# Taking DRAIN instructions out of the PSUM evacuation of a feed-forward stage, and one buffer for its bias broadcast

## The chip, the cores and the metric

The kernel runs on all 8 cores of one Trainium2 chip. Each core handles its own 2048 tokens (half a sequence of one of 4 batch entries), and nothing is exchanged between cores. The metric is the device time in microseconds of the slowest core; lower is better.

## What is computed

A pre-norm transformer layer on x of shape 4 x 4096 x 1024:

```python
x = x + attn(layernorm(x), Wq, Wk, Wv, Wo)        # 16 heads, rotary, full softmax
x = x + ffn(layernorm(x), w1, b1, w2, b2)
# ffn: two "bitlinear" layers, 1024 -> 4096 -> 1024, exact gelu between them
def bitlinear(x, w, b):
    xq = act_quant(rmsnorm(x))      # rounded to -128..127 by the row's max
    wq = weight_quant(w)            # rounded to -1, 0, 1
    return einsum('bsd,fd->bsf', xq, wq) + b
```

## The kernel before, in words

The program is written by hand, with one instruction stream per engine and named semaphores. It has five stages with a barrier of all engines between them (`barrier_all`, line 116): row statistics, the projections to K, Q and V, attention (the exponential at L686), the output projection with the quantization of w2, and the feed-forward stage. Only this last stage is touched. Its code begins at line 1016.

**Where it starts.** b1 (4096 numbers) and b2 (1024) have to stand in all 128 partitions (`b1_bc`, `b2_bc`). This is done in five pieces of 1024 numbers: GpSimd loads a piece of 4 KB to row 0 of `outb` (L1082), TensorE multiplies it by a column of ones (two fp32 matmuls, L1115 and L1118 for even pieces, L1123 and L1126 for odd ones), and VectorE copies the two halves from PSUM (L1138, L1139 or L1142, L1143). Two rows (`outb[0]`, `outb[1]`) and two PSUM places (`ps4_b1`, `ps4_b2`) take turns. GpSimd's stream goes on with the loads of the first tiles of its tokens, `y1t` (512 KB each, L1086 and L1092).

**The loop over 16 token tiles of 128.** For tile t TensorE runs, in this order: 8 transposes of the quantized input of tile t+1 (L1303, "A transposes"), 32 transposes of the quantized hidden row of tile t (L1323, "B transposes"), 64 matmuls of the first layer of tile t+1 (L1290: 8 blocks of 512 columns, 8 matmuls each), 64 matmuls of the second layer of tile t (L1338). All transposes share three PSUM slots, `ps4_tr`: transpose g waits in `wait_slot` until transpose g-3 has been copied out. VectorE copies the A transposes (`ev1_copies`, L1173) and the odd B transposes (`ev2_odd`, L1246), ScalarE the even B transposes (L1385).

VectorE's stream for tile t is: two quantizing passes over a quarter of the hidden row (L1251, L1260), two more, the 8 A copies, 4 odd B copies, a quarter's passes, 4 copies, a quarter's passes, 8 copies; then the output of tile t-1 (`do_out`, L1202); then for each of the 8 blocks of the first layer the scale and bias out of PSUM (`hstt_range`, L1183) and, two blocks behind, the maximum over the block after gelu (`mx8_one`, L1209); then the quantized input of tile t+2 (`q1_round`, L1153 to L1166) and a chain of six small operations. ScalarE runs gelu (L1376) and the sum of squares (L1379) for each block.

**How an instruction tells that it is done.** Nearly everywhere on VectorE and ScalarE the instruction is followed by a separate `e.drain()`, and the semaphore's increment hangs on that drain. A helper such as `ev1_copies` reads

```python
e.wait_ge(SM["pTE"], gq1(t, i) + 1)
e.tensor_copy(q1fm[:, i * 128:(i + 1) * 128], ps4_tr[gq1(t, i) % 3][:])
e.drain().then_inc(SM["vTE"], 1)
```

The exception is the exponential of the attention stage (L686), which carries its increment itself.

Of the kernel before, what the change touches and what calls it, by code (L numbers as in the profile page):

```python
# [11 lines left out]
AF = mybir.ActivationFunctionType  # L12
ALU = mybir.AluOpType
# [16 lines left out]
def build_nc():  # L30
# [14 lines left out]
    b1r = din("b1r", [1, FF])  # L45
    b2r = din("b2r", [1, D])
# [10 lines left out]
    with st_all:  # L57
# [4 lines left out]
        def mkp(stack, name, shape, dtype=F32):  # L62
# [15 lines left out]
            "vQ2", "vQ2c", "pL2", "dBb", "vOU", "dOUa", "dOUb",  # L78
        ]
        SM = {n: st_all.enter_context(nc.semaphore(n)) for n in SEMS}  # L80

# [3 lines left out]
        ones_f1 = mk(st_all, "ones_f1", [1, 128])  # L85
# [941 lines left out]
        ps4_b2 = mkp(st4, "ps4_b2", [128, 1024])  # L1027
# [46 lines left out]

        @block.gpsimd
        def _(e):
            for cc in range(5):
                if cc >= 2:
                    e.wait_ge(SM["pIC"], cc - 1)
                src = (b1r[0:1, cc * 1024:(cc + 1) * 1024] if cc < 4  # L1080
                       else b2r[0:1, :])
                e.dma_start(out=outb[cc % 2][0:1, 0:1024],  # L1082
                            in_=src).then_inc(SM["dB" if cc % 2 == 0
                                                 else "dBb"], 16)
            for t in range(2):
# [20 lines left out]
        @block.tensor  # L1106
        def _(e):
            for cc in range(5):
                e.wait_ge(SM["dB" if cc % 2 == 0 else "dBb"],
                          16 * (cc // 2 + 1))  # L1110
                bdst = b1_bc if cc < 4 else b2_bc
                if cc >= 2:
                    e.wait_ge(SM["vC2"], cc - 1)
                if cc % 2 == 0:
                    e.matmul(ps4_b1[0][:], ones_f1[:],  # L1115
                             outb[0][0:1, 0:512],
                             start=True, stop=True, skip_group_check=True)
                    e.matmul(ps4_b1[1][:], ones_f1[:],  # L1118
                             outb[0][0:1, 512:1024],
                             start=True, stop=True,  # L1120
                             skip_group_check=True).then_inc(SM["pIC"], 1)
                else:
                    e.matmul(ps4_b2[:, 0:512], ones_f1[:],  # L1123
                             outb[1][0:1, 0:512],
                             start=True, stop=True, skip_group_check=True)
                    e.matmul(ps4_b2[:, 512:1024], ones_f1[:],  # L1126
                             outb[1][0:1, 512:1024],
                             start=True, stop=True,
                             skip_group_check=True).then_inc(SM["pIC"], 1)

        @block.vector
        def _(e):
            for cc in range(5):
                e.wait_ge(SM["pIC"], cc + 1)
                bdst = b1_bc if cc < 4 else b2_bc
                off = cc * 1024 if cc < 4 else 0
                if cc % 2 == 0:
                    e.tensor_copy(bdst[:, off:off + 512], ps4_b1[0][:])  # L1138
                    e.tensor_copy(bdst[:, off + 512:off + 1024],  # L1139
                                  ps4_b1[1][:])  # L1140
                else:
                    e.tensor_copy(bdst[:, off:off + 512], ps4_b2[:, 0:512])  # L1142
                    e.tensor_copy(bdst[:, off + 512:off + 1024],  # L1143
                                  ps4_b2[:, 512:1024])
                e.drain().then_inc(SM["vC2"], 1)

        @block.vector
        def _(e):
# [21 lines left out]
            def ev1_copies(t):  # L1170
                for i in range(NDC):
                    e.wait_ge(SM["pTE"], gq1(t, i) + 1)
                    e.tensor_copy(q1fm[:, i * 128:(i + 1) * 128],  # L1173
                                  ps4_tr[gq1(t, i) % 3][:])
                    e.drain().then_inc(SM["vTE"], 1)

            def hstt_range(t, fcs):
                for fc in fcs:
                    g = 8 * t + fc
                    e.wait_ge(SM["pL1"], g + 1)  # L1180
                    if g >= 2:
                        e.wait_ge(SM["aGE"], g - 1)
                    e.scalar_tensor_tensor(hb[g % 2][:], ps4_b1[fc % 2][:],  # L1183
                                           c1o_t[:, t:t + 1],
                                           b1_bc[:, fc * 512:(fc + 1) * 512],
                                           ALU.mult, ALU.add)
                    e.drain().then_inc(SM["vIC"], 1)

            RRS = ["rr", "ssq"]

# [30 lines left out]
            for t in range(NTTQ):  # L1221
# [138 lines left out]
        def _(e):  # L1360
# [9 lines left out]
            for t in range(NTTQ):  # L1370
# [101 lines left out]
```

## Time and profile before

| what | us |
|---|---|
| two runs, lowest and highest | 2822.35 and 2880.93 |
| their median | 2851.64 |
| the profiled execution | 2826.34 |
| its span, slowest core (core 0) | 2824.7 |
| spans of the eight cores | 2804.1 to 2824.7 |
| feed-forward stage of core 0 | about 2070 to 2824.7 |

A row of the timeline gives the start, the duration, the engine, the line, the operation, the output and inputs, how many instructions are merged in the row and, in brackets, how long the engine had been idle and what ended that. PE is TensorE's matmul, PEld its weight load, DVE VectorE, ACT ScalarE, POOL GpSimd. A releaser with a q, such as DVEq, is an instruction of the engine's sequencer, here mostly a drain. "issue" is time in which the engine waited for nothing that the profile shows.

### The profile page before, as it was taken

The page shows a single profiled execution, that of the slowest core. Times are in us where ns is not written, and L with a number is a line of the kernel's source. Part 1 is how long each engine was busy: PE and PEld are TensorE (multiplying, and loading weights), DVE is VectorE, ACT ScalarE, POOL GpSimd, SP SyncE. Part 2 cuts the span into 40 slices and gives each one's busy share as a digit, 9 for nine tenths or more (in the row PEclk, how much of TensorE's full clock was granted, in tenths as well). Part 3 has the DMA queues.
Part 4 walks back from the last instruction along what each step waited for, and adds up shares of the span by engine and source line. Part 5 has one row for each costly group of instructions (what it writes and reads, how often), then busy time and mean ns, then how long its engine had stood idle before and what let it go on. Part 6 is the DMA issues. An engine that isn't in the chain of part 4 may idle for free.

```text
span 2824.7 us, 33066 instructions; the slowest of 8 cores (2804.1 to 2824.7 us)
## 1 busy us (share of the span) xinstructions
PE 2212.6 (78%) x8854; PEld 759.8 (27%) x8940; DVE 1067.9 (38%) x1941; ACT 1600.0 (57%) x2139; POOL 181.1 (6%) x345
## 2 busy tenths in 40 slices
PE   4679999788888888888888888554047888888887
PEld 1223333222222222222222222121013333334333
DVE  2424445401111111101122220188555666666664
ACT  3301111399888999889998889411433443434432
POOL 4211111000000000000000000011110000000000
PEclk8799999898898998888988889777567988889888
DMA  9632323301101010101111110366520000000000
GB/s 159 96 60 60 60 58 72 103 16 30 53 30 45 23 53 31 53 1 45 45 45 62 39 36 6 80 220 207 189 71 16 16 31 16 31 23 23 31 16 23
DMA packets 72194, 160.57 MB, mean 57 GB/s; under 512 B 8144, under 2 KB 41040, under 8 KB 70736
## 3 DMA queue, kind: packets, MB, share of 16 engines
q0 software_dynamic: 48544, 104.90, 16.0%
q1 hardware_dynamic: 23472, 53.55, 5.3%
q8 instruction: 80, 1.31, 0.2%
q14 instruction: 98, 0.80, 0.1%
HBM read 158.42 MB, written 29.36 MB: 66 GB/s over the span
## 4 chain that ended last, share of the span: by engine, by line
PE 40%; ACT 28%; DVE 11%; issue 11%; DMA 6%; DVEq 1%; ACTq 1%; POOL 0%; POOLq 0%; SPq 0%
ACT Et L686 25%; PE ps_b L1290 8%; PE ps_b L1338 8%; PE ps_k L405 5%; PE ps_v L380 4%; PE ps_tr L1323 3%; DMA xb<-x_fm 3%; PE ps_cA L621 2%; PE ps_S L656 2%; PE ps_cB L627 2%; DMA w2st<-w2T 2%; DVE wtmp L878 1%; DVE q1fm L1173 1%; PE ps_k L412 1%; PE ps_n L421 1%
## 5 line engine op out<-in xcount | busy, mean ns | idle before, releaser
L686 ACT ACTIVATE Et<-ps_S,negG 128x1024 bf16<-128x1024 f32 x1024 | 1046.8, 1172 | 85.0 <-PE ps_S L661 77.7
L656 PE MATMUL ps_S<-Qp,Kp 64*128 64x512 bf16 x1024 | 411.7, 407 | 122.9 <-ACT Et L686 72.5
L621 PE MATMUL ps_cA<-Et,V_sb 128*65 128x512 bf16 x1024 | 436.6, 426 | 43.1 <-DVEq L768 36.6
L661 PE MATMUL ps_S<-Qp,Kp 64*128 64x512 bf16 x1024 | 423.3, 418 | 0.0
L627 PE MATMUL ps_cB<-Et,V_sb 128*65 128x512 bf16 x1024 | 413.9, 404 | 0.0
L756 DVE COPY rlbc<-ps_rl 64x512 f32<-64x512 f32 x32 | 21.8, 682 | 768.3 <-PE ps_rl L638 768.3
L1290 PE MATMUL ps_b<-w1q,q1fm 128*128 128x512 bf16 x992 | 251.1, 417 | 7.3 <-issue 5.2
L656 PEld LDWEIGHTS ps_S<-Qp,Kp 64*128 64x128 bf16 x1024 | 93.5, 94 | 597.3 <-issue 597.2
L493 ACT ACTIVATE ksq<-krot 128x512 bf16<-128x512 bf16 x96 | 60.4, 629 | 298.0 <-DVEq L461 298.0
L1338 PE MATMUL ps_b<-w2q,q2fm 128*128 128x512 bf16 x1007 | 225.0, 382 | 3.3 <-DVEq L1205 2.4
L621 PEld LDWEIGHTS ps_cA<-Et,V_sb 128*65 128x65 bf16 x1024 | 113.5, 111 | 301.2 <-issue 294.6
L1385 ACT ACTIVATE q2fm<-ps_tr 128x128 bf16<-128x128 bf16 x256 | 70.9, 277 | 194.3 <-PE ps_tr L1323 193.8
L1323 PE MATMUL ps_tr<-eye_b,h_scb 128*128 128x128 bf16 x512 | 114.9, 252 | 77.3 <-DVEq L1248 51.6
L1290 PEld LDWEIGHTS ps_b<-w1q,q1fm 128*128 128x128 bf16 x1024 | 106.9, 106 | 146.6 <-issue 50.7
L979 PE MATMUL ps_y<-wo_b,ctx_fm 128*128 128x512 bf16 x250 | 80.4, 490 | 74.1 <-DVEq L863 50.3
L1338 PEld LDWEIGHTS ps_b<-w2q,q2fm 128*128 128x128 bf16 x1024 | 100.6, 98 | 124.9 <-issue 5.7
L380 PE MATMUL ps_v<-wv_b,xr 128*128 128x512 bf16 x496 | 115.0, 383 | 18.1 <-DMA xr<-x_fm 16.6
L1183 DVE SCALAR_TENSOR_TENSOR hb<-ps_b,c1o_t,b_bc 128x512 f32<-128x512 f32 x128 | 96.1, 751 | 85.1 <-PE ps_b L1290 66.8
L627 PEld LDWEIGHTS ps_cB<-Et,V_sb 128*65 128x65 bf16 x1024 | 119.3, 117 | 6.6
L405 PE MATMUL ps_k<-xr,wk_b 128*128 128x512 bf16 x504 | 119.8, 381 | 1.3 <-issue 1.3
L596 POOL DMA_DIRECT2D w1st_<-w1T x64 | 33.8, 528 | 1157.2 <-DVEq L716 630.7
L1209 DVE TENSOR_REDUCE mx<-h_sc 128x1 f32<-128x512 f32 x128 | 87.8, 686 | 23.4 <-issue 18.0
(199 smaller groups left out, 2152.5 us busy)
## 6 DMA issues: line engine op xcount, KB each, us to landing
w1st_<-w1T POOLq DMA_DIRECT2D x64, 512.0 KB, 4.2
w2st<-w2T POOLq DMA_DIRECT2D x64, 512.0 KB, 4.6
xb<-x_fm POOLq DMA_DIRECT2D x64, 128.0 KB, 9.6
xr<-x_fm POOLq DMA_DIRECT2D x64, 128.0 KB, 6.0
kscr<-krot SPq DMA_DIRECT2D x64, 128.0 KB, 1.9
Kp<-kscr SPq DMA_DIRECT2D x8, 1024.0 KB, 4.8
xq<-x_tmq SPq DMA_DIRECT2D x16, 512.0 KB, 5.9
y1scr<-y1r SPq DMA_DIRECT2D x16, 512.0 KB, 5.1
```

Source lines behind the costliest of these rows:

```text
L380: e.matmul(ps1_v[j % 2][:, h * 512:(h + 1) * 512], xr[bi % 2][:, c * 512 + t4 * 128: c * 512 + t4 * 128 + 128], wv_b[:, c * 1024 + h * 512 ...
L405: mm = e.matmul(ps1_k[idx % 2][:], wb[:, c * 1024 + mdo * 128:c * 1024 + mdo * 128 + 128], xr[bi % 2][:, c * 512:(c + 1) * 512], start=(c ...
L621: e.matmul(ps2_cA[:], V_sb[:, jj * VBLK + (2 * m) * VW: jj * VBLK + (2 * m) * VW + VW], Et[itp % 4][:, 0:512], start=(jj == 0), stop=(jj = ...
L627: e.matmul(ps2_cB[:], V_sb[:, jj * VBLK + (2 * m + 1) * VW: jj * VBLK + (2 * m + 1) * VW + VW], Et[itp % 4][:, 512:1024], start=(jj == 0), ...
L656: e.matmul(ps2_S[it % 2][:, 0:512], Kp[m % 2][0:64, j * 128:(j + 1) * 128], Qp[m % 2][0:64, qh * 512:(qh + 1) * 512], start=True, stop=Tru ...
L661: e.matmul(ps2_S[it % 2][:, 512:1024], Kp[m % 2][64:128, j * 128:(j + 1) * 128], Qp[m % 2][64:128, qh * 512:(qh + 1) * 512], start=True, s ...
L686: e.activation(Et[it % 4][:], ps2_S[it % 2][:], AF.Exp, bias=negG[:, m:m + 1], scale=1.0).then_inc(SM["aEX"], 1)
L1183: e.scalar_tensor_tensor(hb[g % 2][:], ps4_b1[fc % 2][:], c1o_t[:, t:t + 1], b1_bc[:, fc * 512:(fc + 1) * 512], ALU.mult, ALU.add)
L1209: e.reduce_max(mx8[:, fc:fc + 1], h_sc[:, fc * 512:(fc + 1) * 512], axis=AX, apply_absolute_value=True)
L1290: last = e.matmul(ps4_b1[fc % 2][:], q1fm[:, c * 128:(c + 1) * 128], w1q[:, c * FF + fc * 512:c * FF + (fc + 1) * 512], start=(c == 0), st ...
L1323: e.transpose(ps4_tr[g % 3][:], h_scb2[k % 2][:, (i % 8) * 128: (i % 8 + 1) * 128], eye_b[:]).then_inc(SM["pTE"], 1)
L1338: last = e.matmul(ps4_b2[:, h2 * 512:(h2 + 1) * 512], q2fm[:, fc * 128:(fc + 1) * 128], w2q[:, fc * 1024 + h2 * 512: fc * 1024 + (h2 + 1) ...
```

## The change

Three things, all in the feed-forward stage.

1. The drain is removed after the A copies, the odd and the even B copies and the `hstt_range` operation, and the increment is put on the operation itself; behind `mx8_one`'s reduction, which carries none, the drain goes without replacement. Over 16 tiles that is 128 drains after A copies, 256 after odd B copies, 128 after L1183 and 128 after L1209 on VectorE, and 256 after even B copies on ScalarE.
2. The bias pieces use `outb[0]` and `ps4_b1` alone. The load of piece cc waits until VectorE has copied piece cc-1 out of PSUM (`vC2`).
3. The first two loads of `y1t` stand ahead of the bias loads in GpSimd's stream.

```diff
@@ gpsimd
-            for cc in range(5):
-                if cc >= 2:
-                    e.wait_ge(SM["pIC"], cc - 1)
...
-                e.dma_start(out=outb[cc % 2][0:1, 0:1024],
-                            in_=src).then_inc(SM["dB" if cc % 2 == 0
-                                                 else "dBb"], 16)
             for t in range(2):
                 e.dma_start(out=y1t[t % 3][:],
...
+            for cc in range(5):
+                if cc >= 1:
+                    e.wait_ge(SM["vC2"], cc)
...
+                e.dma_start(out=outb[0][0:1, 0:1024],
+                            in_=src).then_inc(SM["dB"], 16)
@@ tensor
-                e.wait_ge(SM["dB" if cc % 2 == 0 else "dBb"],
-                          16 * (cc // 2 + 1))
+                e.wait_ge(SM["dB"], 16 * (cc + 1))
-                if cc >= 2:
-                    e.wait_ge(SM["vC2"], cc - 1)
...
@@ ev1_copies (the same in ev2_odd, in hstt_range and in ScalarE's copy)
                     e.tensor_copy(q1fm[:, i * 128:(i + 1) * 128],
-                                  ps4_tr[gq1(t, i) % 3][:])
-                    e.drain().then_inc(SM["vTE"], 1)
+                                  ps4_tr[gq1(t, i) % 3][:]
+                                  ).then_inc(SM["vTE"], 1)
@@ mx8_one
                 e.reduce_max(mx8[:, fc:fc + 1],
                              h_sc[:, fc * 512:(fc + 1) * 512], axis=AX,
                              apply_absolute_value=True)
-                e.drain()
```

On GpSimd, at the start of the stage, the loads stand in this order before; `outb0` and `outb1` are the two bias rows, `pIC` counts pieces that TensorE has multiplied.

```order
L1075 UNCONDITIONAL_BRANCH [waits sBAR]
L1082 DMA outb0<-b1r 1x16x64
L1082 DMA outb1<-b1r 1x16x64
L1082 DMA outb0<-b1r 1x16x64 [waits pIC]
L1082 DMA outb1<-b1r 1x16x64 [waits pIC]
L1082 DMA outb0<-b2r 1x16x64 [waits pIC]
L1086 DMA y1t0<-y1scr 128x1024
L1086 DMA y1t1<-y1scr 128x1024
L1092 DMA y1t2<-y1scr 128x1024
```

The same place of the changed kernel; `vC2` counts pieces that VectorE has copied out.

```order
L1075 UNCONDITIONAL_BRANCH [waits sBAR]
L1078 DMA y1t0<-y1scr 128x1024
L1078 DMA y1t1<-y1scr 128x1024
L1086 DMA outb0<-b1r 1x16x64
L1086 DMA outb0<-b1r 1x16x64 [waits vC2] x3
L1086 DMA outb0<-b2r 1x16x64 [waits vC2]
L1091 DMA y1t2<-y1scr 128x1024
```

Two large loads have moved ahead of the bias, and four of the five bias loads now wait for VectorE instead of three for TensorE.

On TensorE, at the same place, the broadcasts before alternate between two PSUM places:

```order
L1106 UNCONDITIONAL_BRANCH [waits sBAR]
L1115 MATMUL ps4_b10<-outb0,ones_f1 128x512 [waits dB]
L1118 MATMUL ps4_b11<-outb0,ones_f1 128x512
L1123 MATMUL ps4_b2<-outb1,ones_f1 128x512 [waits dBb]
L1126 MATMUL ps4_b2<-outb1,ones_f1 128x512
L1115 MATMUL ps4_b10<-outb0,ones_f1 128x512 [waits dB,vC2]
L1118 MATMUL ps4_b11<-outb0,ones_f1 128x512
```

and in the changed kernel every piece goes through the same one:

```order
L1110 MATMUL ps4_b10<-outb0,ones_f1 128x512 [waits dB]
L1112 MATMUL ps4_b11<-outb0,ones_f1 128x512
L1110 MATMUL ps4_b10<-outb0,ones_f1 128x512 [waits dB]
L1112 MATMUL ps4_b11<-outb0,ones_f1 128x512
L1110 MATMUL ps4_b10<-outb0,ones_f1 128x512 [waits dB]
```

The number of matmuls is the same; each pair waits for a load that is itself behind the copies of the pair before. In the loop over tiles no instruction other than the drains changes its place on any engine.

## Rows read from the trace of the kernel before

**Rows 1.** TensorE's timeline through one tile; start, duration, instruction, idle before.

```profile
2493.90 15.79 PE L1290 MATMUL ps_b<-w1q,q1fm 128*128 128x512 bf16 x62 [0.36 <-issue]
...
2523.34 0.33 PE L1303 MATMUL ps_tr<-eye_b,uscr_b 128*128 128x128 bf16 x3
...
2524.48 0.22 PE L1303 MATMUL ps_tr<-eye_b,uscr_b 128*128 128x128 bf16 x1 [0.19 <-DVEq L1175]
...
2530.99 2.12 PE L1323 MATMUL ps_tr<-eye_b,h_scb 128*128 128x128 bf16 x8 [1.54 <-DVEq L1248]
...
2538.19 2.34 PE L1290 MATMUL ps_b<-w1q,q1fm 128*128 128x512 bf16 x5 [0.34 <-issue]
```

**Rows 2.** Windows: stretch, its length, busy time by engine, TensorE's granted clock, DMA.

```profile
2070.00:2092.00 22.00, 17.40 (x20) 6.33 (x20) 6.73 (x11) 0.00 (x0) 4.03 (x8) 0.50 0.21 72
...
2523.30:2538.20 14.90, 8.71 (x42) 4.02 (x42) 8.29 (x28) 4.43 (x16) 0.00 (x0) 0.68 0.00 1
```

**Rows 3.** VectorE's timeline between the matmuls of that tile.

```profile
2523.66 0.23 DVE L1173 COPY q1fm<-ps_tr 128x128 bf16<-128x128 bf16 x1 [0.45 <-PE ps_tr L1303]
...
2524.08 0.22 DVE L1173 COPY q1fm<-ps_tr 128x128 bf16<-128x128 bf16 x1 [0.19 <-issue]
...
2524.49 0.22 DVE L1173 COPY q1fm<-ps_tr 128x128 bf16<-128x128 bf16 x1 [0.19 <-PE ps_tr L1303]
...
2528.45 0.23 DVE L1246 COPY q2fm<-ps_tr 128x128 bf16<-128x128 bf16 x1 [0.21 <-PE ps_tr L1323]
...
2528.80 0.75 DVE L1251 TENSOR_SCALAR h_sc<-h_sc,scr 128x1024 f32<-128x1024 f32 x1
```

**Rows 4.** Timeline of the w2 quantization: two operations with a drain between, GpSimd behind them.

```profile
2057.77 0.69 DVE L932 TENSOR_SCALAR w2st<-w2st 128x1024 f32<-128x1024 f32 x1 [1.18 <-ACTq L967]
2058.55 0.70 DVE L935 TENSOR_SCALAR w2q<-w2st 128x1024 bf16<-128x1024 f32 x1
...
2059.82 0.53 POOL L829 DMA_DIRECT2D w2st<-w2T  x1 [2.12 <-DVEq L937]
```

**Rows 5.** Timeline of the bias broadcast: GpSimd, TensorE, VectorE.

```profile
2070.68 0.98 POOL L1082 DMA_DIRECT2D outb<-b1r  x2 [7.65 <-DVEq L119]
...
2072.72 2.04 PE L1115 MATMUL ps_b<-outb,ones_f 1*128 1x512 f32 x2 [88.16 <-DMA outb<-b1r]
...
2076.58 0.69 DVE L1138 COPY b_bc<-ps_b 128x512 f32<-128x512 f32 x1 [6.59 <-PE ps_b L1118]
...
2077.19 0.68 DVE L1139 COPY b_bc<-ps_b 128x512 f32<-128x512 f32 x1
...
2091.71 0.55 DVE L1153 TENSOR_SCALAR uscr<-y1t,c1q_t,kmag_t 128x512 f32<-128x512 f32 x1 [0.19 <-issue]
```

**Rows 6.** Costliest groups: the exponential, whose increment is on the instruction itself.

```profile
L686 ACT ACTIVATE Et<-ps_S,negG 128x1024 bf16<-128x1024 f32 x1024 | 1046.8, 1172 | 85.0 <-PE ps_S L661 77.7
```

**Rows 7.** Attention stage's timeline: two exponentials and the matmul that waits for the second.

```profile
999.06 2.15 ACT L686 ACTIVATE Et<-ps_S,negG 128x1024 bf16<-128x1024 f32 x2
...
1001.36 0.37 PE L656 MATMUL ps_S<-Qp,Kp 64*128 64x512 bf16 x1
```

**Rows 8.** The two loads of line 1086, from issue to landing.

```profile
DMA to landing us min/median/max: 3.6/4.3/5.0
```

**Rows 9.** Where weight loads become dense again after three starts of matmuls (with those starts).

```profile
2098.92 15.50 PE L1290 MATMUL ps_b<-w1q,q1fm 128*128 128x512 bf16 x62 [1.11 <-DVEq L1175]
...
2102.18 10.03 PEld L1290 LDWEIGHTS ps_b<-w1q,q1fm 128*128 128x128 bf16 x47 [0.16 <-issue]
...
2137.68 3.57 PE L1290 MATMUL ps_b<-w1q,q1fm 128*128 128x512 bf16 x8
...
2143.10 7.22 PEld L1290 LDWEIGHTS ps_b<-w1q,q1fm 128*128 128x128 bf16 x34 [0.20 <-issue]
...
2498.09 9.38 PEld L1290 LDWEIGHTS ps_b<-w1q,q1fm 128*128 128x128 bf16 x44 [0.20 <-issue]
```

**Rows 10.** TensorE's timeline: its wait for VectorE in the first tile.

```profile
2123.84 1.91 PE L1303 MATMUL ps_tr<-eye_b,uscr_b 128*128 128x128 bf16 x5 [9.24 <-DVEq L1175]
```

More of the change, by code:

```diff
@@ L77, in build_nc @@
             "vQ1", "pTE", "vTE", "vTEB", "vTEBD", "pL1", "aGE", "aSQ", "vSF", "aC2", "vC2",
-            "vQ2", "vQ2c", "pL2", "dBb", "vOU", "dOUa", "dOUb",
+            "vQ2", "vQ2c", "pL2", "vOU", "dOUa", "dOUb",
         ]
@@ L1076, in _ @@
         def _(e):
-            for cc in range(5):
-                if cc >= 2:
-                    e.wait_ge(SM["pIC"], cc - 1)
-                src = (b1r[0:1, cc * 1024:(cc + 1) * 1024] if cc < 4
-                       else b2r[0:1, :])
-                e.dma_start(out=outb[cc % 2][0:1, 0:1024],
-                            in_=src).then_inc(SM["dB" if cc % 2 == 0
-                                                 else "dBb"], 16)
             for t in range(2):
@@ L1088, in _ @@
                             ).then_inc(SM[["dYLa", "dYLb", "dYLc"][t % 3]], 16)
+            for cc in range(5):
+                if cc >= 1:
+                    e.wait_ge(SM["vC2"], cc)
+                src = (b1r[0:1, cc * 1024:(cc + 1) * 1024] if cc < 4
+                       else b2r[0:1, :])
+                e.dma_start(out=outb[0][0:1, 0:1024],
+                            in_=src).then_inc(SM["dB"], 16)
             for t in range(2, NTTQ):
@@ L1108, in _ @@
             for cc in range(5):
-                e.wait_ge(SM["dB" if cc % 2 == 0 else "dBb"],
-                          16 * (cc // 2 + 1))
+                e.wait_ge(SM["dB"], 16 * (cc + 1))
                 bdst = b1_bc if cc < 4 else b2_bc
-                if cc >= 2:
-                    e.wait_ge(SM["vC2"], cc - 1)
[L1114 to L1129, printed above, removed]
+                e.matmul(ps4_b1[0][:], ones_f1[:], outb[0][0:1, 0:512],
+                         start=True, stop=True, skip_group_check=True)
+                e.matmul(ps4_b1[1][:], ones_f1[:], outb[0][0:1, 512:1024],
+                         start=True, stop=True,
+                         skip_group_check=True).then_inc(SM["pIC"], 1)
         @block.vector
@@ L1136, in _ @@
                 off = cc * 1024 if cc < 4 else 0
[L1137 to L1144, printed above, removed]
+                e.tensor_copy(bdst[:, off:off + 512], ps4_b1[0][:])
+                e.tensor_copy(bdst[:, off + 512:off + 1024], ps4_b1[1][:])
                 e.drain().then_inc(SM["vC2"], 1)
@@ L1185, in hstt_range @@
                                            b1_bc[:, fc * 512:(fc + 1) * 512],
-                                           ALU.mult, ALU.add)
-                    e.drain().then_inc(SM["vIC"], 1)
+                                           ALU.mult,
+                                           ALU.add).then_inc(SM["vIC"], 1)
             RRS = ["rr", "ssq"]
@@ L1246, in ev2_odd @@
                         e.tensor_copy(q2fm[:, i * 128:(i + 1) * 128],
-                                      ps4_tr[gq2(t, i) % 3][:])
-                        e.drain().then_inc(SM["vTEBD"], 1)
+                                      ps4_tr[gq2(t, i) % 3][:]
+                                      ).then_inc(SM["vTEBD"], 1)
                 for k in range(4):
@@ L1385, in _ @@
                     e.activation(q2fm[:, i * 128:(i + 1) * 128],
-                                 ps4_tr[gq2(t, i) % 3][:], AF.Copy)
-                    e.drain().then_inc(SM["vTEB"], 1)
+                                 ps4_tr[gq2(t, i) % 3][:],
+                                 AF.Copy).then_inc(SM["vTEB"], 1)
         @block.sync
@@ L1393, in _ @@
             e.wait_ge(SM["dYLc"], 16 * 5)
-            e.wait_ge(SM["dB"], 16 * 3)
-            e.wait_ge(SM["dBb"], 16 * 2)
+            e.wait_ge(SM["dB"], 16 * 5)
         st4.close()
```

## The prediction

> **What bounds the kernel now.** I read the timeline of one late tile first, engine by engine, then the windows for TensorE's clock, then the start of the feed-forward stage. Everything before that stage is untouched, so only the last 750 us count.
>
> A tile takes 2538.19 - 2493.90 = 44.3 us from first matmul to first matmul [rows 1]. TensorE multiplies without a break from 2493.90 to 2523.34, 29.4 us, and then needs 14.85 us for 40 transposes. The reader should see that the second part is not TensorE's own work: single transposes stand 0.2 to 1.5 us apart and a DVE drain released them. The mechanism is the ring of three PSUM slots: a transpose may start only when the one three before it has been copied out. Behind the first three transposes the copies on VectorE follow each other every 0.41 us, 0.22 of copy and 0.19 in which the engine idles with "issue" as its reason, that is, for its own drain and the wait instruction behind it [rows 3]. TensorE then waits 1.54 us for the first odd B copy after two quantizing passes [rows 1, 3].
>
> TensorE's granted clock is part of this. In the transposes it is 0.68 on average [rows 2]: at 2.4 GHz for (0.68 - 0.5) / 0.5 = 36% of 14.9 us, so it falls to 1.2 GHz about 5.4 us after the matmuls end, and the next matmuls begin at 1.2 GHz and regain 2.4 GHz only 4.2 us later, where the weight loads become dense (2493.90 to 2498.09) [rows 1, 9].
>
> The start of the stage is a chain of its own: from the first bias load at 2070.68 to the end of the last bias copy, just before 2091.71, about 20.8 us [rows 5], at 1.2 GHz throughout [rows 2]. TensorE is busy for 17.4 of these 22 us: the two PSUM places keep it fed, and loads and copies lie beside it. No tile can start before it.
>
> **The change part by part.**
>
> *The bias in one buffer.* Now each piece runs load, multiply, copy, and only then the next load. From rows 5: GpSimd's issue to TensorE's start 2072.72 - 2070.68 = 2.04; TensorE's start to VectorE's first copy 2076.58 - 2072.72 = 3.86; the two copies start 0.61 apart and the second takes 0.68, 1.29 together. From VectorE's end to a load on GpSimd that waits for its drain: 2059.82 - (2058.55 + 0.70) = 0.57 [rows 4]. One round is 2.04 + 3.86 + 1.29 + 0.57 = 7.76; a later load may land a tenth or two sooner, so I take 7.7. Four rounds are 30.8, and the fifth piece ends with 3.86 + 1.29 = 5.15.
>
> *The y1t loads ahead of it.* They cost their issue on GpSimd, two of about 0.55 us, and perhaps their transfer. From the stage's start to the first bias matmul: at least 1.1 + 2.04 = 3.1 us if the small load passes them, and 0.55 + 5.0 + 0.1 = 5.7 if it lands behind the second large one [rows 8]. There the third large load was competing, so I take 5.0. The new start is then 5.0 + 30.8 + 5.15 = 41 us against 20.8: **+20 us**, with bounds +16 (first load early, rounds 7.2) and +23. Nothing hides it: VectorE's bias copies stand ahead of the first tile in its stream. The early y1t saves nothing, since tile 0 did not wait for it: its first operation followed the copies by 0.19 of issue [rows 5].
>
> The page DMA: Bandwidth & Descriptors of the Trainium skill (Queues, rings and completion order) says that a semaphore write of a DMA engine lands only behind that engine's earlier writes, across its queues. By that rule the small load is counted behind both large ones, which is the upper of my two ends; no row of this trace has a small load issued behind large ones on the same queue.
>
> *The A copies.* What does a copy without its drain cost? The same engine shows both forms on plain operations: with a drain between them L932 and L935 start 0.78 apart at a duration of 0.69 [rows 4]; the bias copies L1138 and L1139, with neither drain nor wait, start 0.61 apart at 0.69 [rows 5], so the second starts 0.08 before the first ends. A wait between two instructions need not break this: the exponentials on ScalarE carry their own increments, have two waits between them, and two of 1.17 us each take 2.15 together [rows 6, 7]. So the 0.19 gap should go. Then the slot ring sets the pace: copy 0.22, copy's end to the next transpose 0.15, transpose's start to its copy 2523.66 - 2523.34 = 0.32 [rows 1, 3], together 0.70 for three slots, 0.23 each. The 0.15 is from the exponential to the matmul it releases, 1001.36 - (999.06 + 2.15) [rows 7]; with a drain it is 2524.48 - 2524.30 = 0.18 [rows 1, 3]. Eight A copies save 8 x (0.41 - 0.23) = 1.4 us per tile. What is late next is the ring itself.
>
> *The odd and even B copies.* Here 8 transposes already take 2.12 us, 0.265 each [rows 1]: the ring binds, not the drains. The shorter handshake saves 0.03 / 3 = 0.01 on each, for some 20 of them 0.2. At two places per tile VectorE goes from an odd copy to the quantizing pass on which the next transposes depend; that gap, 2528.80 - 2528.68 = 0.12 [rows 3], turns into an overlap of 0.08: 2 x 0.2 = 0.4.
>
> Sum per tile: 1.4 + 0.2 + 0.4 = **2.0 us**. From both sides: 0 if wait and increment take as long as the drain did, and 8 x (0.41 - 0.14) + 0.4 + 0.5 = 3.0 if copies could run at 0.22 - 0.08 = 0.14 without regard to the ring. I take 2.0 because both terms are read at this very place.
>
> *L1183 and L1209.* Their drains stand while TensorE multiplies without a break, so that TensorE hides whatever they save in 15 tiles. If that cover were gone, it would be 0.2 x 16 = 3.2 us a tile, but it would need TensorE to wait in the matmuls, and it doesn't. Tile 0 is different: no second-layer matmuls cover VectorE there, and TensorE waits 9.24 us [rows 10]. I put the saving at 1.4 (0.9 because the last L1183 no longer trails, and three gaps of 0.15 to 0.2).
>
> *The clock.* The matmuls will start 2 us sooner, but whether 2.4 GHz returns sooner too is open: after three starts it came back after 3.3, 5.4 and 4.2 us [rows 1, 9]. A microsecond more at 1.2 GHz costs half of one. I subtract 0.3 per tile; the spread of the three, 3.3 to 5.4 against 4.2, allows -0.45 to +0.6.
>
> **Sum.** 15 tile intervals x (2.0 - 0.3) = 25.5; tile 0 another 1.4, its first A copies 1.4, the last tile (B transposes only) 0.6: 28.9 saved, 20 added, **-9 us**. The profiled execution took 2826.34, its span 2824.7. Forecast: 2826.3 - 9 = **2817 us**. That execution lies near the lower of the two runs shown (2822.35 and 2880.93) and 25 us below their median; the forecast is for an execution like it.
>
> **The rivals.**
>
> *The drains were free.* Wait and increment may take their 0.19 anyway, and the copies keep their pace. For it: no row shows VectorE with an increment on the operation and a wait behind it. Against it: rows 6 and 7 on ScalarE, and 0.61 against 0.78 in rows 5 and 4. Then only the bias chain is left, with handshakes saving some 2 us: 2826.3 + 20 - 2 = 2844, slower than before. It decides wherever the saving stays under 1.2 us per tile, which is the 20 us over 16.5 tiles. The Trainium skill's page VectorE: DVE Perf Modes (The DRAIN you can't avoid) states this very case: eight copies took the same time with a semaphore after each as with one after the last, since each operation drains anyway. The bias copies, 0.61 apart, don't show such a wait; by that rule the result would be this rival's.
>
> *The clock keeps half.* If 2.4 GHz returns at the moment it would have returned anyway, 2 us more at 1.2 GHz give back 1.0 a tile: 15 x 1.0 + 3.4 = 18.4 saved, 2826.3 + 20 - 18.4 = 2828. For it: the three returns do not follow the start by one fixed time. Against: nothing ties them to a place in the old schedule.
>
> *The clock stays up.* If the denser transposes kept 2.4 GHz, each start would save 4.2 / 2 = 2.1 more: 15 x (2.0 + 2.1) + 3.4 = 65, 2826.3 + 20 - 65 = 2781. Against it: in the last third of the gap 8 transposes still take about 2 us and VectorE's passes still leave TensorE idle for over a microsecond twice.
>
> **How the numbers follow.** Forecast 0.5, drains free 0.18, clock keeps half 0.2, clock stays up 0.05, and 0.07 for an execution like the higher of the two shown. The bounds of the terms give 2826 + 23 - 0 = 2849 as the slow end and 2826 + 16 - (15 x 3.0 + 5) = 2792 as the fast one; with part of the spread of the two runs above it the range is **2796 to 2860**. Within 2% (about what a measurement of this kernel can tell from no change) lie all cases but a part of the last two: 0.94. Faster 0.03, slower 0.03.
>
> **What would show it.** Right: five bias rounds of about 7.7 us with GpSimd's loads waiting for VectorE, the first tile starting 20 us later; A copies 0.23 apart with TensorE as their releaser; the B ring still near 0.26; tiles 42 to 43 us apart; a granted clock that still falls to 0.5 in every gap. Wrong: copies still 0.41 apart (drains free), tiles of 43.3 or more with the first matmuls at 0.5 for over 5.5 us (the clock's share), tiles near 40 with no 0.5 (the clock stays up), or a bias start under 36 us.

## The result and the profile after

| what | us |
|---|---|
| changed kernel, median of 24 runs (lowest, highest) | 2811.7 (2799.6, 2883.6) |
| kernel before, median of 23 runs beside them | 2826.4 |
| ratio of the two, with its 95% interval | 0.9938 (0.9913 to 0.9962) |
| that ratio in us | -17.5 (-24.6 to -10.7) |
| profiled execution of the changed kernel | 2808.8 |
| forecast | 2817, which is -9 |

It is a little faster and within 2%, as forecast, but by about twice as much. Medians and extremes are over all runs; some runs, of the kernel before too, are a few per cent longer at a lower granted clock on one die or both, and the ratios, and the times given for e4 and e7 below, leave those out. The profile says where the gain lies. The slowest core is now core 3:

```profile
span 2807.2 us, 32253 instructions; the slowest of 8 cores (2785.5 to 2807.2 us)
```

All rows below are of core 0 where nothing else is said, so that they can be laid beside the rows of before. Line numbers have moved: the bias loads are now L1086, the bias copies L1122 and L1123, the first operation of a tile L1132, the A copies L1152, the odd and even B copies L1224 and L1363, the transposes L1281 (A) and L1301 (B), the first-layer matmuls L1268.

**The start.** The timeline of GpSimd, TensorE and VectorE answers to [rows 5]:

```profile
2069.10 1.05 POOL L1078 DMA_DIRECT2D y1t<-y1scr  x2 [7.46 <-DVEq L119]
2070.14 0.50 POOL L1086 DMA_DIRECT2D outb<-b1r  x1
2074.35 2.04 PE L1110 MATMUL ps_b<-outb,ones_f 1*128 1x512 f32 x2 [90.36 <-DMA outb<-b1r]
...
2078.20 0.69 DVE L1122 COPY b_bc<-ps_b 128x512 f32<-128x512 f32 x1 [9.77 <-PE ps_b L1112]
...
2080.08 0.49 POOL L1086 DMA_DIRECT2D outb<-b1r  x1 [9.44 <-DVEq L1124]
2082.05 2.04 PE L1110 MATMUL ps_b<-outb,ones_f 1*128 1x512 f32 x2 [3.96 <-DMA outb<-b1r]
...
2110.08 0.55 DVE L1132 TENSOR_SCALAR uscr<-y1t,c1q_t,kmag_t 128x512 f32<-128x512 f32 x1 [0.19 <-issue]
```

GpSimd's second bias load is released by VectorE's drain (DVEq L1124), and TensorE, which was busy almost throughout before, waits 3.96 us for it. The first matmul comes 5.25 us after the first issue (forecast 5.0), the second round starts 7.70 later (7.7; the other three take 7.52, 7.57 and 7.60), and the first tile begins 2110.08 - 2069.10 = 41.0 us after the first issue (41). Against 21.0 before that is 20 us lost, on all eight cores (20.9 to 22.2 before, 40.8 to 41.7 now).

**Between the matmuls.** The timeline of one late tile, TensorE and VectorE together, answers to [rows 1] and [rows 3]:

```profile
2517.67 0.33 PE L1281 MATMUL ps_tr<-eye_b,uscr_b 128*128 128x128 bf16 x3
2517.99 0.49 DVE L1152 COPY q1fm<-ps_tr 128x128 bf16<-128x128 bf16 x3 [2.09 <-PE ps_tr L1281]
...
2518.36 0.48 PE L1281 MATMUL ps_tr<-eye_b,uscr_b 128*128 128x128 bf16 x3 [0.37 <-DVE q1fm L1152]
2518.68 0.49 DVE L1152 COPY q1fm<-ps_tr 128x128 bf16<-128x128 bf16 x3 [0.21 <-PE ps_tr L1281]
...
2519.06 0.35 PE L1281 MATMUL ps_tr<-eye_b,uscr_b 128*128 128x128 bf16 x2 [0.21 <-DVE q1fm L1152]
2519.38 0.36 DVE L1152 COPY q1fm<-ps_tr 128x128 bf16<-128x128 bf16 x2 [0.20 <-PE ps_tr L1281]
...
2521.50 0.23 DVE L1224 COPY q2fm<-ps_tr 128x128 bf16<-128x128 bf16 x1 [0.33 <-PE ps_tr L1301]
2521.64 0.74 DVE L1229 TENSOR_SCALAR h_sc<-h_sc,scr 128x1024 f32<-128x1024 f32 x1
...
2523.78 0.52 PE L1301 MATMUL ps_tr<-eye_b,h_scb 128*128 128x128 bf16 x3 [1.42 <-DVE q2fm L1224]
...
2530.61 14.78 PE L1268 MATMUL ps_b<-w1q,q1fm 128*128 128x512 bf16 x62 [0.34 <-issue]
```

Three copies of 0.22 now stand in one row of 0.49, so they start 0.13 apart, and then VectorE waits for TensorE, not for itself. The groups of three start at 2517.99, 2518.68 and 2519.38: the ring of three slots turns in 0.69 to 0.70 us, the 0.70 of the forecast. Behind an odd copy the quantizing pass starts 0.09 before the copy ends (forecast 0.08). The gap is 2530.61 - 2517.67 = 12.94. Its mean over tiles 2 to 14 is 12.85 against 14.82, on every core within 0.02: **1.97 us shorter, forecast 2.0**. The means here and below run from the first weight load of the A transposes to the first of the matmuls, because on two cores, core 0 among them, some matmul rows are missing (x62 of 64).

**The clock.** Windows of 100 us from the middle of the stage, after and then before (columns as in [rows 2]; the last but two is TensorE's granted clock):

```profile
2300.00:2400.00 100.00, 86.13 (x389) 39.38 (x393) 62.02 (x151) 41.13 (x101) 1.05 (x2) 0.86 0.06 22
2400.00:2500.00 100.00, 86.91 (x388) 39.91 (x396) 61.78 (x140) 44.24 (x106) 1.58 (x3) 0.85 0.09 32
2500.00:2600.00 100.00, 89.64 (x411) 41.24 (x418) 65.79 (x147) 44.31 (x105) 1.05 (x2) 0.90 0.06 22
```

```profile
2300.00:2400.00 100.00, 83.03 (x367) 37.24 (x371) 63.06 (x143) 39.18 (x98) 1.05 (x2) 0.84 0.06 22
2400.00:2500.00 100.00, 84.88 (x362) 37.60 (x369) 61.83 (x135) 40.33 (x97) 1.58 (x3) 0.82 0.09 32
2500.00:2600.00 100.00, 86.83 (x382) 38.73 (x388) 64.53 (x134) 45.58 (x109) 1.05 (x2) 0.86 0.06 22
```

The clock has become better, 0.87 against 0.84 in the mean, where I had counted a loss. Counted over whole tiles (2 to 14, all cores), TensorE is at 1.2 GHz for 11.3 us of a tile against 13.6. How much of it falls into the matmuls can be read, as in [rows 9], from a start of matmuls and the place where the weight loads become dense. After, three neighbouring tiles:

```profile
2404.52 14.68 PE L1268 MATMUL ps_b<-w1q,q1fm 128*128 128x512 bf16 x62 [0.34 <-issue]
2406.23 12.47 PEld L1268 LDWEIGHTS ps_b<-w1q,q1fm 128*128 128x128 bf16 x58 [0.28 <-issue]
...
2445.75 14.51 PE L1268 MATMUL ps_b<-w1q,q1fm 128*128 128x512 bf16 x54 [0.34 <-issue]
2450.81 9.16 PEld L1268 LDWEIGHTS ps_b<-w1q,q1fm 128*128 128x128 bf16 x43 [0.22 <-issue]
...
2488.84 15.18 PE L1268 MATMUL ps_b<-w1q,q1fm 128*128 128x512 bf16 x62 [0.34 <-issue]
2491.77 11.75 PEld L1268 LDWEIGHTS ps_b<-w1q,q1fm 128*128 128x128 bf16 x55 [0.22 <-issue]
```

1.7, 5.1 and 2.9 us. Counted instead from the first weight load, which lies 0.4 us ahead of these matmul rows, to the clock's own record, it is 2.3, 5.4 and 3.3 us. By this count the matmuls spend 2.0 to 5.6 us at 1.2 GHz over tiles 2 to 14 of all cores, 3.5 in the mean; before it was 2.8 to 4.6, 4.2 in the mean, and 4.1 to 4.6 from tile 6 on. A tile now takes 41.98 us (mean of tiles 2 to 14 over the cores) against 44.30: 1.97 from the gap and 0.35 from the matmuls (0.5 on core 0).

### The profile page after: what moved, and what is told of

Its sections match the earlier page's. It is cut to its first block, busy times and chain, and to the rows that moved or that the text cites. A ratio compares the mean times of both kernels' runs of the same rounds, so it can differ in the third digit from the quotient of the medians.

```text
span 2807.2 us, 32253 instructions; the slowest of 8 cores (2785.5 to 2807.2 us)
## 1 busy us (share of the span) xinstructions
PE 2210.7 (79%) x8940; PEld 758.7 (27%) x8940; DVE 1040.4 (37%) x1941; ACT 1602.7 (57%) x2139; POOL 180.7 (6%) x345
## 3 DMA queue, kind: packets, MB, share of 16 engines
q8 instruction: 80, 1.31, 0.2%
## 4 chain that ended last, share of the span: by engine, by line
PE 43%; ACT 29%; DVE 10%; issue 10%; DMA 6%; DVEq 1%; ACTq 1%; POOL 0%; POOLq 0%; SPq 0%
ACT Et L686 25%; PE ps_b L1268 9%; PE ps_b L1316 8%; PE ps_k L405 6%; PE ps_v L380 4%; PE ps_tr L1301 3%; PE ps_cA L621 3%; PE ps_S L656 2%; PE ps_cB L627 2%; DMA xb<-x_fm 2%; DMA w2st<-w2T 2%; DVE wtmp L878 1%; PE ps_k L412 1%; PE ps_n L421 1%; DVE h_scb L1238 1%
## 5 line engine op out<-in xcount | busy, mean ns | idle before, releaser
L621 PE MATMUL ps_cA<-Et,V_sb 128*65 128x512 bf16 x1024 | 436.4, 426 | 43.8 <-DVEq L768 37.1
L1268 PE MATMUL ps_b<-w1q,q1fm 128*128 128x512 bf16 x1024 | 253.0, 413 | 0.7 <-DVE q1fm L1152 0.6
L1363 ACT ACTIVATE q2fm<-ps_tr 128x128 bf16<-128x128 bf16 x256 | 69.9, 278 | 190.9 <-PE ps_tr L1301 187.4
L1301 PE MATMUL ps_tr<-eye_b,h_scb 128*128 128x128 bf16 x512 | 105.6, 248 | 69.3 <-DVE q2fm L1224 44.5
L1268 PEld LDWEIGHTS ps_b<-w1q,q1fm 128*128 128x128 bf16 x1024 | 106.0, 105 | 142.5 <-issue 40.5
L1110 PE MATMUL ps_b<-outb,ones_f 1*128 1x512 f32 x10 | 10.2, 1121 | 105.9 <-DMA outb<-b1r 102.1
```

The costliest lines, as they stand in the source:

```text
L621: e.matmul(ps2_cA[:], V_sb[:, jj * VBLK + (2 * m) * VW: jj * VBLK + (2 * m) * VW + VW], Et[itp % 4][:, 0:512], start=(jj == 0), stop=(jj = ...
L1268: last = e.matmul(ps4_b1[fc % 2][:], q1fm[:, c * 128:(c + 1) * 128], w1q[:, c * FF + fc * 512:c * FF + (fc + 1) * 512], start=(c == 0), st ...
L1301: e.transpose(ps4_tr[g % 3][:], h_scb2[k % 2][:, (i % 8) * 128: (i % 8 + 1) * 128], eye_b[:]).then_inc(SM["pTE"], 1)
```

## The experiments

My theory after the result: (a) the bias chain costs its 20 us; (b) the drains are worth 2.0 us of gap per tile, because VectorE stood still behind each and the three-slot ring now sets the pace; (c) the rest, some 0.35 us per tile, is the clock, which follows the rhythm of the loop and not the length of the gap alone. The rivals: the drains cost through the late signal and not through the standstill; the saving comes from L1183 and L1209; part of the start's cost is not the chain but the loads ahead of it; the clock takes back what the gap gives. A ratio is given where a kernel ran often enough for one (e1, e2, e8, e12); the others stand on one execution each. "Gap" is from the first A transpose to the first matmul, by their weight loads, "tile" the time from one tile's first matmul to the next one's, in the mean of tiles 2 to 14.

### e1 and e2: the two halves of the change apart

e1 is the changed kernel with all drains back:

```diff
-                                  ps4_tr[gq1(t, i) % 3][:]
-                                  ).then_inc(SM["vTE"], 1)
+                                  ps4_tr[gq1(t, i) % 3][:])
+                    e.drain().then_inc(SM["vTE"], 1)
...
```

> Kernel before with the change's bias start alone (one buffer, loads waiting for VectorE, y1t first), all drains kept. Theory (two parts that add): from the first load of the stage to the first L1153-type operation 40 to 41 us instead of 21, then the tiles exactly as before, 44.3 to 44.4 us each; the time about 19 to 20 us above the kernel before, ratio 1.007. Rival (the drains were free and the saving comes from elsewhere, say from the new start moving the tiles against TensorE's clock): the tiles themselves get shorter than 44 us here, and the ratio stays below 1.003.

Measured: 2848.6 us beside 2827.5, ratio 1.0068 (1.0037 to 1.0099), so +19 us; start 40.8 to 42.1, gap 14.82, tiles 44.26 to 44.38 as before.

e2 is the kernel before with the drains taken out and its bias chain left alone.

> Kernel before with the drains removed alone, its own bias start kept. Theory: start 21 us as before, tiles 41.9 us on average as in the changed kernel, the stage some 39 us shorter than before: about 2787 us against 2826, ratio 0.986. Rival (part of the gain needs the other start): tiles above 43 us, ratio above 0.990. This is also the version that should beat both.

Measured: 2786.8 us, ratio 0.9854 (0.9809 to 0.9899), -41 us; start 20.9 to 22.1, gap 12.82 to 12.87, tiles 41.86 to 42.14. The halves add up, 19 - 41 = -22, inside the interval of the whole. (a) stands, and "the drains were free" falls.

### e3, e4 and e5: which drains

e3 takes the drains away after the A copies alone, e4 after the B copies alone, e5 at L1183 and L1209 alone (each the kernel before with one or two hunks of the diff).

> Kernel before with the drain removed behind the A copies only (L1173, 8 per tile). The stretch between the matmuls should shrink from 14.85 to about 13.4 us, copies 0.25 apart. Theory that the stretches add up: tiles 44.4 - 1.4 = 43.0 us, stage 22 us shorter. Rival (TensorE's clock takes it back: its return to 2.4 GHz stays where it was, so the next matmuls run longer at 1.2 GHz): with half given back tiles of 43.7; with all of it, as long as every tile keeps the same cold stretch, tiles stay at 44.4, the time at 1.2 GHz after the matmuls' start growing from 4.3 toward 7 us.

> Kernel before with the drains removed behind the B copies only (L1246 and L1385, 32 per tile). The stretch between the matmuls should shrink by 0.5 to 0.7 us, from 14.85 to about 14.2: two gaps in front of the quantizing passes and a slightly shorter handshake in the slot ring. Theory that the stretches add up: tiles 43.8 us, stage 9 to 10 us shorter. Rival (the clock takes it back): tiles stay at 44.4 us, with about 1.2 us more at 1.2 GHz after the start of the matmuls, and the time is that of the kernel before.

> Kernel before with the drains removed only behind L1183 and L1209, which stand while TensorE multiplies without a break. Theory (TensorE hides them): stretch between the matmuls still 14.8 us, tiles 1 to 15 still 44.3 to 44.4 us; only tile 0, where TensorE waits for VectorE, is 1.0 to 1.4 us shorter. Rival (VectorE sets the pace of the matmuls too): tiles shorter by up to 3 us.

| | us | gap | tile |
|---|---|---|---|
| before | 2826 | 14.82 | 44.30 |
| e3, A copies | 2804.9 | 13.52 (-1.30) | 42.85 |
| e4, B copies | 2811.3 | 14.15 (-0.67) | 43.63 |
| e5, L1183 and L1209 | 2824.2 | 14.83 | 44.38 |

The two gaps add up to the whole, 1.30 + 0.67 = 1.97, against 1.4 and 0.6 in the forecast. In e3 and e4 the matmuls took 29.3 and 29.5 us, so the clock took nothing back. In e5 the tiles stay because VectorE waits there for TensorE. The timeline in the first-layer matmuls of e5:

```profile
2450.59 0.75 DVE L1183 SCALAR_TENSOR_TENSOR hb<-ps_b,c1o_t,b_bc 128x512 f32<-128x512 f32 x1 [0.38 <-PE ps_b L1289]
2451.26 0.68 DVE L1209 TENSOR_REDUCE mx<-h_sc 128x1 f32<-128x512 f32 x1
```

and the same place before:

```profile
2504.93 0.75 DVE L1183 SCALAR_TENSOR_TENSOR hb<-ps_b,c1o_t,b_bc 128x512 f32<-128x512 f32 x1 [0.22 <-issue]
2505.86 0.69 DVE L1209 TENSOR_REDUCE mx<-h_sc 128x1 f32<-128x512 f32 x1 [0.19 <-issue]
```

The 0.22 and 0.19 behind the drains have gone, and the pair starts to start takes 1.73 us instead of 1.85, TensorE's pace. The interval of tile 0, for which I had counted 1.4 us, shortened by 0.1 on core 0 and by 0.7 in the mean over the cores (from 0.2 longer to 1.8 shorter). But TensorE was at 1.2 GHz for 11.1 us of it in the mean, against 9.2 before, so this one execution doesn't tell the drains' share from the clock's.

### e6: the bias loads in front again

```diff
-            for t in range(2):
-                e.dma_start(out=y1t[t % 3][:], ...
             for cc in range(5):
...
+            for t in range(2):
+                e.dma_start(out=y1t[t % 3][:], ...
```

> The changed kernel with the five bias loads put ahead of the first two y1t loads again. Theory (the small load is counted only behind the two large ones): first bias matmul 2.0 us after the first issue instead of 5.3, rounds of 7.5 to 7.7 unchanged, so the start is 3.2 us shorter; y1t of tile 0 lands behind the last round and costs nothing or at most 2 us. Rival (only the two issues cost): the start is 1.1 us shorter.

```profile
2062.36 0.50 POOL L1082 DMA_DIRECT2D outb<-b1r  x1 [7.38 <-DVEq L119]
```

```profile
2064.24 2.04 PE L1110 MATMUL ps_b<-outb,ones_f 1*128 1x512 f32 x2 [86.30 <-DMA outb<-b1r]
```

Measured: 2807.3 us beside 2825.8. The first bias matmul comes 1.88 us after the issue, where it came 2074.35 - 2070.14 = 4.2 after its own issue behind the two large loads. The start takes 37.5 to 38.8 us, in the mean over the cores 3.1 fewer. So 3.1 of the 20 us are the loads ahead, and 16.7 the chain. The Trainium skill's page DMA: Bandwidth & Descriptors (Queues, rings and completion order) would have the small load counted behind the large ones. These two runs agree: its landing is seen 4.1 us after its issue behind them and 1.8 without them. They don't tell this rule from a load whose data simply waited its turn.

### e7: the increment on the copy, and a drain behind it

It is the changed kernel with `e.drain()` added behind each of the five operations. The signal goes out with the copy, but the engine still stands still.

```diff
                                   ).then_inc(SM["vTE"], 1)
+                    e.drain()
```

> The changed kernel with its increments left on the operations, but a drain put behind each again. It separates the late signal from the engine that stands still. Theory (it is the engine's gap that costs): A copies 0.39 to 0.41 apart again and the stretch between the matmuls 14.5 to 14.8 us, a few tenths of the 2.0 kept for the earlier signal; tiles 44 us. Rival (it is the signal's path through the drain): the stretch stays near 12.9 us and the tiles near 42.

The timeline of VectorE and TensorE in the A transposes:

```profile
2478.73 0.22 DVE L1152 COPY q1fm<-ps_tr 128x128 bf16<-128x128 bf16 x1 [0.16 <-issue]
2479.12 0.22 DVE L1152 COPY q1fm<-ps_tr 128x128 bf16<-128x128 bf16 x1 [0.16 <-PE ps_tr L1285]
```

```profile
2479.11 0.22 PE L1285 MATMUL ps_tr<-eye_b,uscr_b 128*128 128x128 bf16 x1 [0.17 <-DVE q1fm L1152]
```

Measured: 2834.8 us; gap 14.29 to 14.33, tiles 43.8 to 44.0. TensorE is now released by the copy itself, but the copies are still 0.39 apart with "issue" behind the first. Of the 1.97 us the earlier signal is worth 0.5, the standstill 1.5. I had expected a gap of 14.5 to 14.8, so the signal is worth a little more than I thought.

### e8 and e9: is the ring what sets the pace now?

e8 is e2 with a fourth PSUM slot. Its place comes from the scratch of the sum of squares, which ScalarE now writes to `h_scb2[1]`. e9 has the four slots and all the drains of before.

```diff
-        ps4_tr = [mkp(st4, f"ps4_tr{i}", [128, 128], BF16) for i in range(3)]
-        ps4_sq = mkp(st4, "ps4_sq", [128, 512])
+        ps4_tr = [mkp(st4, f"ps4_tr{i}", [128, 128], BF16) for i in range(4)]
...
-            if g < 3:
+            if g < 4:
...
-            kind, ci = GKIND[g - 3]
+            kind, ci = GKIND[g - 4]
```

> The drains-only kernel with four PSUM slots for the transposes instead of three; the bank comes from the scratch of ScalarE's sums of squares, which goes to an idle half of h_scb2. Theory (without drains the slot ring sets the pace): A copies 0.18 to 0.20 apart instead of 0.25, B transposes 0.20 instead of 0.24 to 0.26, the stretch between the matmuls 10.8 to 11.3 us instead of 12.85, tiles about 40 us, the time about 2758 us, ratio 0.976. Rival (the copies themselves or TensorE's pace at 1.2 GHz bind): the stretch stays above 12.4 us and the ratio at 0.984 to 0.986.

> The kernel before, drains kept, with the four slots. With run e8 it gives all four corners of drains and slots. Theory (with its drains VectorE sets the pace of the A copies, the ring that of the B copies): A copies still 0.41 apart, B transposes 0.20 to 0.22 instead of 0.265, the stretch between the matmuls 13.6 to 14.0 us instead of 14.8; tiles about 43.4. So the fourth slot gives 1 us with drains and gave 2.5 us without. Rival (the slots give the same in both): stretch 12.3 us.

Timeline of the A transposes in e8:

```profile
2476.37 0.39 PE L1301 MATMUL ps_tr<-eye_b,uscr_b 128*128 128x128 bf16 x4
2476.70 1.31 DVE L1172 COPY q1fm<-ps_tr 128x128 bf16<-128x128 bf16 x8 [2.10 <-PE ps_tr L1301]
```

and in e9:

```profile
2467.18 0.23 DVE L1172 COPY q1fm<-ps_tr 128x128 bf16<-128x128 bf16 x1 [0.19 <-issue]
2467.59 0.22 DVE L1172 COPY q1fm<-ps_tr 128x128 bf16<-128x128 bf16 x1 [0.19 <-PE ps_tr L1302]
```

| gap, us | 3 slots | 4 slots |
|---|---|---|
| drains | 14.82 | 13.49 |
| no drains | 12.85 | 10.37 |

Measured: e8 2744.7 us, ratio 0.9706 (0.9688 to 0.9725), tiles 39.40 to 39.59; e9 2802.5 beside 2822.4, tiles 42.7. Without drains the eight A copies run in one row of 1.31 us, 0.16 apart; with them the fourth slot changes nothing at this place, the copies stay 0.41 apart. The same drains are worth 1.97 us with three slots and 3.12 with four: each of the two bounds hides part of the other. Both gaps came out below what I had expected (10.8 to 11.3 and 13.6 to 14.0). Moving the scratch is not what did it: e11 below moves it too, with three slots, and its gap is 12.92.

### e10, e11 and e12: what the clock is worth

These add matmuls to the B transposes whose results nothing uses: e10, on top of e2, five before the 13th and the 21st, where TensorE waits for VectorE; e11 four there and one before every other second transpose; e12 is e8 with the added matmuls of e11, in a PSUM place of the first layer that is free then.

```diff
+                    for _f in range(4 if i in (12, 20) else (1 if i % 2 == 0 else 0)):
+                        e.matmul(ps4_fill[:], eye_b[:], w1q[:, 0:512],
+                                 start=True, stop=True,
+                                 skip_group_check=True)
                     g = gq2(t, i)
```

> The drains-only kernel with ten added matmuls per tile that compute nothing that is used (eye times a stretch of w1q into the bank that the squares left), five before the transposes 12 and 20, where TensorE waits 1.4 us for VectorE. It asks what TensorE's clock costs. Theory (half of the time at 1.2 GHz behind the matmuls' start is lost): if the filling keeps the clock at 2.4 GHz, matmuls of a tile take 27.4 to 27.6 us instead of 29.1 and the tile about 40.5 us instead of 42.0; if the clock still falls, the filling costs up to 0.7 us at each place and the tile is 42 to 43.5. Rival (the clock in the matmuls' start doesn't matter): tiles not below 42 in either case.

> As the run before, with four such matmuls before the transposes 12 and 20 and one before every second of the 32 transposes, so that TensorE is busy through the whole stretch. Theory: more likely than the other to keep 2.4 GHz through the stretch; the filling itself costs 0.2 us where a transpose was not waiting, some 1 to 2 us a tile, against 1.7 us won in the matmuls: tiles 41 to 42.5. Rival: the clock falls all the same, and tiles are 44 or more.

> e8 (four slots, no drains) with the added matmuls of e11 put before its B transposes (one before every second, four before the 13th and the 21st), into a PSUM place of the first layer that is free there; their results are used by nothing. In e8 a tile took 39.4 to 39.6 us: a gap of 10.37 and 29.1 of matmuls, of which on average 3.3 at 1.2 GHz. In e11 the granted clock stayed at 2.4 GHz through all tiles: matmuls 27.0 to 27.6, gap 12.6. If the clock is a cost of its own that stands beside the ring's, the two savings add: gap 10.4 to 11.0 (the small added matmuls of 0.22 may delay a transpose), matmuls 27.4, tiles 37.8 to 38.4, and about 2745 - 15 x 1.4 = 2724 us (2712 to 2732), ratio to before 0.964. If the transposes in four slots have no room for them, each pair of transposes is delayed by 0.1 to 0.2 us, the gap is 12 or more, tiles are 39.4 and the time is that of e8, 2745. If the clock falls all the same, it is above 2750.

Windows of e10, e11 and e12 at the same stretch:

```profile
2400.00:2500.00 100.00, 92.81 (x431) 42.16 (x430) 63.33 (x145) 44.68 (x109) 1.58 (x3) 0.93 0.09 32
```

```profile
2400.00:2500.00 100.00, 94.88 (x470) 43.62 (x469) 66.71 (x144) 48.65 (x113) 1.58 (x3) 1.00 0.09 33
```

```profile
2400.00:2500.00 100.00, 94.67 (x491) 45.97 (x499) 69.74 (x166) 46.49 (x113) 1.06 (x2) 1.00 0.06 22
```

| | us | ratio to before | tile, core 0 |
|---|---|---|---|
| e2 | 2786.8 | 0.9854 | 42.1 |
| e10 | 2769.2 | one execution | 41.3 |
| e11 | 2759.6 | one execution | 40.4 |
| e8 | 2744.7 | 0.9706 | 39.4 |
| e12 | 2727.4 | 0.9648 (0.9630 to 0.9666) | 38.1 |

In e11 and e12 the granted clock stays at 2.4 GHz from the second tile on to the last ones; in e10 it still falls, for a shorter time (0.93 here, 0.88 in e2). In e11 and e12 the 64 + 64 matmuls take 27.4 us, counted between weight loads like the gap (29.1 in e8, 29.5 before). The gap grows little for the added ones: to 12.92 in e11 from 12.85, to 10.61 in e12 from 10.37. Between the matmul rows, one tile of e12 has 2466.09 - 2455.77 = 10.32, where e8 has 10.17 in the mean of core 0.

```profile
2455.77 0.39 PE L1301 MATMUL ps_tr<-eye_b,uscr_b 128*128 128x128 bf16 x4
...
2466.09 13.97 PE L1288 MATMUL ps_b<-w1q,q1fm 128*128 128x512 bf16 x63
```

So the clock cost 29.5 - 27.4 = 2.1 us per tile before and costs 29.1 - 27.4 = 1.7 in the changed kernel. For e11 I had expected the added matmuls to cost 1 to 2 us and tiles of 41 to 42.5; they cost 0.1, and e11's tiles are shorter than e2's by 1.6 us in the mean over the cores. e12 beats both kernels by the widest margin. Its expectation (tiles of 37.8 to 38.4, 2724 us) held: the savings of the ring and of the clock add up.

## Why the prediction was right in direction and too small

| step | forecast | measured, core 0 |
|---|---|---|
| start: first bias matmul / round / all | 5.0 / 7.7 / 41 us | 5.25 / 7.5 to 7.7 / 41.0 |
| cost of the start | 20 | 20.0 |
| gap per tile | -2.0 | -1.97 |
| clock per tile | +0.3 | -0.5 (mean of the cores -0.35) |
| first tile's A copies | -1.4 | -1.3 |
| interval of tile 0 | -3.1 | -2.9 |
| last tile | -0.6 | -1.6 |
| all behind the start | -28.9 | -40.7 |

**Right.** The bias start came out to the microsecond, including the choice of the upper end for the load behind two large ones. The A copies were slowed by their own drains and are now by the ring, at the 0.70 us that [rows 1], [rows 3] and [rows 7] gave. L1183 and L1209 are hidden, "the drains were free" is refuted by e2, and the clock still falls to 0.5 in every gap, so "the clock stays up" did not come by this change (e11 shows it can: 27.4 us of matmuls against 29.5 before, the 2.1 worked out).

I read too much into the Trainium skill's page VectorE: DVE Perf Modes (The DRAIN you can't avoid). Its pair of measurements compares semaphores after each copy with one after the last; it does not speak of a drain instruction in the program, and the same section says that a next operation that is not held starts earlier. In this case's trace the copies start 0.13 apart at 0.22 of duration once the drain instructions are gone, which agrees with that last sentence and not with a pipeline that must be empty first, and the kernel is 41 us shorter in e2.

**Wrong: the clock term, in its sign.** I wrote "I subtract 0.3 per tile". Measured, the matmuls gained 0.35 in the mean over the cores (0.5 on core 0). The mean lay in the spread I gave (-0.45 to +0.6), but on its other side. The difference of 0.8 x 15 = 12 us on core 0 is the whole miss between 28.9 and 40.7, and 0.65 x 15 = 10 over the cores is about the miss in the total, -17.5 against -9. The three returns of [rows 9], 3.3 to 5.4 us, all came from core 0, two of them from its first tiles. The other cores would have warned me. Core 4 of before, two starts and returns:

```profile
2126.64 15.34 PE L1290 MATMUL ps_b<-w1q,q1fm 128*128 128x512 bf16 x64
...
2170.55 15.32 PE L1290 MATMUL ps_b<-w1q,q1fm 128*128 128x512 bf16 x64
```

```profile
2129.05 8.73 PEld L1290 LDWEIGHTS ps_b<-w1q,q1fm 128*128 128x128 bf16 x41 [0.17 <-issue]
...
2173.40 10.24 PEld L1290 LDWEIGHTS ps_b<-w1q,q1fm 128*128 128x128 bf16 x48 [0.20 <-issue]
```

2.4 and 2.85 us, so the loop can come back to 2.4 GHz much sooner than 4.2, and the 4.1 to 4.6 of all late tiles of before was a state of that rhythm and no price of every start. Once the tile was shorter the returns spread over 2.0 to 5.6 with a lower mean, 3.5. e3 (2.1 to 5.5, mean 3.8) and e4 (2.1 to 5.4, mean 4.1) spread too, while e1 and e5, whose tiles keep their 44.3 us, kept before's value (means 4.2 and 4.3). The mean need not fall: in e7, with tiles of 44.0, it is 4.6.

The windows between two changes of the clock show something that I had overlooked. Before, and then after:

```profile
2498.00:2528.72 30.72, 28.51 (x134) 13.01 (x134) 20.64 (x44) 14.99 (x32) 0.00 (x0) 1.00 0.05 17
2528.72:2542.37 13.65, 9.57 (x33) 3.95 (x34) 7.62 (x18) 3.33 (x12) 0.53 (x1) 0.50 0.11 41
```

```profile
2396.13:2406.37 10.24, 6.04 (x25) 2.95 (x27) 5.88 (x16) 2.76 (x11) 0.07 (x1) 0.50 0.00 1
2406.37:2437.09 30.72, 29.38 (x140) 13.57 (x141) 20.25 (x45) 15.00 (x32) 0.46 (x1) 1.00 0.10 35
2437.09:2450.74 13.65, 9.71 (x35) 4.16 (x36) 7.02 (x18) 4.02 (x13) 0.53 (x1) 0.50 0.19 62
```

In the late tiles of every kernel without added matmuls the stretch at 2.4 GHz lasts 30.7 us; the stretch at 1.2 GHz takes the rest of the tile, 13.6 us of 44.3 before, and now 10.2 in some tiles and 13.7 in others, 11.3 in the mean. So a shorter tile loses its time at 1.2 GHz, 1.6 us of it in the gap and 0.7 in the matmuls. Why the other stretch keeps its length, and how a tile's 1.2 GHz divides between gap and matmuls, was not tried and stays open; both are gone in e11 and e12.

Two smaller terms are less sure: the tile-0 share of L1183 and L1209 (1.4, against 0.1 on core 0 and 0.7 over the cores in e5), and the last tile (0.6 against 1.6, where the stretch at 1.2 GHz behind its transposes lasts 10.2 us instead of 13.7 on every core).

## What to carry to other kernels

Put the increment on the operation and leave out the explicit drain wherever the next instruction of that engine doesn't need the result, above all in short copies that hand PSUM slots back; then give the ring one more slot, since each of the two hides part of the other's worth. A bias broadcast in one buffer with loads behind large ones costs as a serial chain (here 20 us, half of what the drains gave), so keep its two buffers and issue small loads first. Where TensorE's granted clock falls in every gap of a loop, read its return in many tiles and on several cores before pricing it, and try a few matmuls in the gap whose results nothing uses.

## What the runs showed of the hardware that I had not expected

- The stretch at 1.2 GHz behind the start of the matmuls is no constant of a gap: 4.1 to 4.6 us in every late tile at 44.3 us per tile, 2.0 to 5.6 at 42, 1.7 to 5.2 in e8 at 39.4, none in e11 and e12.
- 22 added matmuls in the gap of a tile lengthened it by 0.1 to 0.2 us and shortened the tile by 1.6 us (e11 against e2) and by 1.4 on top of four slots (e12 against e8), because the granted clock stayed at 2.4 GHz.
- Three quarters of the price of this loop's drains is the standstill of their own engine (1.5 of 1.97 us per tile), not the later signal (e7).
- VectorE's copies of 128 x 128 start as little as 0.13 us apart at 0.22 us each, with a wait on a semaphore between them.
